# Scores and transposed scores of banded attention on two halves of TensorE's rows

## The reference, cut to what matters

```python
qkv = jnp.einsum('btc,oc->bto', x, w_qkv)
q, k, v = (heads(q), heads(k), heads(v))
attn = jnp.einsum('bhqd,bhkd->bhqk', q, k) / math.sqrt(DK)     # DK = 8
mask = jnp.abs(idx[None, :] - idx[:, None]) > WINDOW           # WINDOW = 128
attn = jnp.where(mask[None, None], -1000000000.0, attn)
p = jax.nn.softmax(attn, axis=-1)
out = jnp.einsum('bhqk,bhkd->bhqd', p, v)
```

## Time and profile before

| | |
|---|---|
| median of 3 runs | 1789.28 us |
| the profiled execution's own time | 1788.06 us |
| its span, first to last instruction | 1786.3 us |
| PE busy | 1529.7 us (86%) |
| DVE busy | 1484.7 us (83%) |
| ACT busy | 1265.5 us (71%) |
| POOL busy | 1328.8 us (74%) |
| mean granted clock of TensorE, of full speed | 0.963 |

### The profile page before, as it was taken

The page is one execution under the profiler, slowest core; times in us unless marked ns, Lnnn a source line. Parts: engine busy times, 40 slices in busy tenths (PEclk is TensorE's granted clock), DMA queues, the critical chain, the costliest instruction groups (busy, mean ns, idle before and its releaser), DMA issues.

```text
span 1786.3 us, 37722 instructions
## 1 busy us (share of the span) xinstructions
PE 1529.7 (86%) x11712; PEld 1086.0 (61%) x11712; DVE 1484.7 (83%) x3720; ACT 1265.5 (71%) x1741; POOL 1328.8 (74%) x1579
## 2 busy tenths in 40 slices
PE   3899999999999999868888888888888888888887
PEld 2456555555565556436666666666666666666666
DVE  3768888887888887339999999989899899899998
ACT  1156666666666666648888888888798888888885
POOL 1145555555555555649999999999999999999993
PEclk9789999999999999969999999999999999999999
DMA  5334444444444443110000000000000000000000
GB/s 139 84 83 93 103 98 97 97 96 96 105 96 96 98 104 75 40 40 1 19 19 1 19 18 6 12 18 18 1 18 18 8 11 18 18 0 18 13 7 7
DMA packets 73406, 85.14 MB, mean 48 GB/s; under 512 B 9856, under 2 KB 63616, under 8 KB 68608
## 3 DMA queue, kind: packets, MB, share of 16 engines
q1 hardware_dynamic: 73312, 84.08, 20.1%
HBM read 58.10 MB, written 25.95 MB: 47 GB/s over the span
## 4 chain that ended last, share of the span: by engine, by line
issue 20%; POOL 20%; DVE 7%; ACT 6%; PE 3%; DVEq 0%; POOLq 0%; ACTq 0%; SPq 0%
POOL SUM L751 20%; DVE W L944 5%; ACT E L852 4%; PE WT L1012 1%; ACT L786 1%; DVE M8Y L888 1%; PE MB L979 1%; PE E L967 1%; ACT GE L785 0%; DVE SMALL L905 0%; DVE CT L927 0%; ACT SIM L779 0%; ACT L785 0%; PE MB L954 0%; DVE Z L911 0%
## 5 line engine op out<-in xcount | busy, mean ns | idle before, releaser
L751 POOL TENSOR_TENSOR SUM<-SIM 128x1024 f32<-128x1024 f32 x512 | 958.3, 1920 | 16.5 <-DVE W L944 12.5
L944 DVE SCALAR_TENSOR_TENSOR W<-SUM,SMALL,E 128x1024 f32<-128x1024 f32 x512 | 642.7, 1280 | 52.3 <-ACT E L852 48.2
L852 ACT ACTIVATE E<-SUM,NB 128x1024 f32<-128x1024 f32 x512 | 567.4, 1118 | 112.8 <-DVE W L944 102.5
L1012 PEld LDWEIGHTS WT<-idf,W 128*128 128x128 f32 x4096 | 473.7, 146 | 263.3 <-DVE W L944 141.3
L1012 PE MATMUL WT<-idf,W 128*128 128x128 f32 x4096 | 552.6, 284 | 90.2 <-DVE CT L927 50.7
L264 POOL TENSOR_SCALAR_AFFINE_SELECT PT<-PT 128x128 f32<-128x128 f32 (+1 forms) x1024 | 334.5, 351 | 315.9 <-ACT PT L354 279.4
L409 DVE TENSOR_REDUCE mx<-SX 128x2 f32<-128x512 f32 x256 | 175.3, 685 | 104.7 <-PE SX L492 104.0
L411 DVE TENSOR_REDUCE mx<-SY 128x2 f32<-128x768 f32 x256 | 242.5, 947 | 6.8 <-PE SY L492 6.2
L354 ACT ACTIVATE PT<-TX 128x512 f32<-128x512 f32 x256 | 152.9, 597 | 95.7 <-PE TX L519 94.1
L356 ACT ACTIVATE PT<-TY 128x768 f32<-128x768 f32 x256 | 207.2, 809 | 1.4
L488 PE MATMUL SY<-K,Q 72*128 72x384 bf16 x512 | 163.2, 341 | 17.2 <-DVE mx L411 16.6
(11 more groups left out here) (111 smaller groups left out, 1663.1 us busy)
## 6 DMA issues: line engine op xcount, KB each, us to landing
K<-k_parts SPq DMA_DIRECT2D x96, 192.0 KB
Q<-q_parts SPq DMA_DIRECT2D x288, 64.0 KB
q_parts<-qp SPq DMA_DIRECT2D x16, 384.0 KB, 2.4
k_parts<-kp SPq DMA_DIRECT2D x16, 384.0 KB, 2.4
xin<-in_x SPq DMA_DIRECT2D x16, 256.0 KB, 3.1
xres<-in_x SPq DMA_DIRECT2D x16, 256.0 KB, 9.4
x<-X SPq DMA_DIRECT2D x16, 256.0 KB, 2.2
x2T<-X2T SPq DMA_DIRECT2D x16, 256.0 KB, 2.1
```

The source lines that it names most:

```text
L751: return eng.tensor_tensor(SUM[(q * FH + h) % RING][:, :].rearrange("p (i j) -> p i j", i=NK), sx, sy, ALU.add)
L852: nc.scalar.activation(E[h % 2][:, :], SUM[(k * FH + h) % RING][:, :], ACT.Exp, bias=NB[q][:, h:h + 1]).then_inc(S["exp_ready"], 1)
L944: nc.vector.scalar_tensor_tensor(out=W[h % WRING][:, :], in0=SUM[(k * FH + h) % RING][:, :], scalar=TOP[q][:, h, TOPK - 1:TOPK], in1=E[h % ...
L1012: o = pe.matmul(WT[:, e, :], W[h % WRING][:, e * P:(e + 1) * P], ident[:, :], is_transpose=True, start=(h == 0 and e % 4 == 0), stop=(h == ...
```

## The change: two halves of the array, other loads, other queues

- A product is taken as 6 terms, not 9 (the parts whose orders add up to two at most), so a score tile contracts over 48 rows, and the transposed one over 51.
- Q and K hold these 48 rows twice, from row 0 and from row 64. The scores of SX and of SY's first tile contract over the upper rows (0 to 47), the transposed scores and SY's second tile over the lower (64 to 114). `heads` writes the matmuls of both in turns. Each mask product over 128 rows becomes two over 64 rows: for SX two of 192 columns on the upper half, for SY two of 2 x 128 columns on each half.
- `values` is cut in four: at each head one of the four spans, 4 matmuls. VSLOT, ASLOT and SHARED move with it.
- SP stores each row where a load wants it (`store_rows`, 3 DMAs for q and 3 for k, 768 KB each, where there was 1 of 384 KB each), and a half is loaded by 4 DMAs of 48 rows, 384 KB each.
- The rows of maxima are stored and loaded from ScalarE's queue, the store one head before the load. `shift` is cut in pieces that lie one head apart. ScalarE now runs a head's exponentials ahead of the other work of that head, and the two short `pow`s of GpSimd lie one head later. `x2_stats` (L468 before) moves to head 1 of the next step.
- The loop of steps begins one step later, with a body of two steps as before.

```diff
-TERMS = 9
-KQ = TERMS * DK
+TERMS = ((0, 3), (1, 2), (2, 1))
+KQ = DK * sum(n for _, n in TERMS)
 SHIFT = 3
+HALF = P // 2
+LOADS = 16 * 4
+STORES = 16 * len(TERMS)
 HT = H // 2 * TILES
 TWO_ONES = float(np.array([0x3F803F80], np.uint32).view(np.float32)[0])
 SLOT_V = 32
 SLOT_PT = 1280
-VSLOT = ((6, 1), (10, 1), (14, 1), (2, 2))
-ASLOT = (3, 8)
+VSLOT = ((4, 1), (8, 1), (12, 1), (0, 2))
+ASLOT = (6, 8)
...
-    SHARED = [(1, "mt1", -1, "max_rest", 2, 2), (3, "att0", -2, "att_normed", 2, 1), (4, "xnT", 1, "xnT_ready", 1, 1),
-              (5, "q", 1, "q_rest", 1, 1), (7, "k", 1, "k_rest", 1, 1), (8, "att1", -2, "att_normed", 2, 2),
+    SHARED = [(1, "mt1", -1, "max_rest", 2, 2), (4, "xnT", 1, "xnT_ready", 1, 1), (5, "q", 1, "q_rest", 1, 1),
+              (6, "att0", -2, "att_normed", 2, 1), (7, "k", 1, "k_rest", 1, 1), (8, "att1", -2, "att_normed", 2, 2),
...
+            for r in (0, HALF):
+                sp.dma_start(K[b][r:r + KQ, hs, :], k_rows[:, hs, :]).then_inc(to, 16)
+                sp.dma_start(Q[b][r:r + KQ, hs, :], q_rows[:, hs, :]).then_inc(to, 16)
+        def store_rows(parts, rows, copies, done):
+            at = 0
+            for e, n in TERMS:
+                src = parts[:, e:e + 1, :].broadcast_to([P, n, T]) if copies else parts[:, 0:n, :]
+                sp.dma_start(rows[at:at + DK * n].rearrange("(a d) h n -> (d h) a n", a=n), src).then_inc(done, 16)
+                at += DK * n
...
-            if 0 <= c - 1 < SEQS:
-                await_(sp, S["max_part3"], (t - 1) * 2 + 2)
-                shift_rows(t - 1, 1, (c - 1) % 2)
...
-            for a in range(3):
-                sp.dma_start(K[b][24 * a:24 * a + 24, hs, :],
-                             k_parts.rearrange("a (d h) n -> (a d) h n", h=H)[:, hs, :]).then_inc(to, 16)
-                for e in range(3):
-                    r = 24 * a + 8 * e
-                    sp.dma_start(Q[b][r:r + 8, hs, :],
-                                 q_parts[a].rearrange("(d h) n -> d h n", h=H)[:, hs, :]).then_inc(to, 16)
...
+                store_rows(qp, q_rows, True, S["q_stored"])
...
+                store_rows(kp, k_rows, False, S["k_stored"])
+                await_(sp, S["q_stored"], STORES * (t + 2))
+                await_(sp, S["k_stored"], STORES * (t + 2))
...
-                if h == 1 and 0 <= c + 1 < SEQS:
+                if h == 2 and 0 <= c + 1 < SEQS:
...
-                if h == 13 and 0 <= c - 2 < SEQS:
+                if h == 14 and 0 <= c - 2 < SEQS:
...
-                    shift(t - 1, 2)
+                    shift_part1(t - 1, 2)
+                if h == 2 and 0 <= c - 1 < SEQS:
+                    shift_part2(t - 1, 2)
                 if h == 9 and 0 <= c < SEQS:
-                    shift(t, 1)
+                    shift_part1(t, 1)
+                if h == 10 and 0 <= c < SEQS:
+                    shift_part2(t, 1)
+                if h == 3 and 0 <= c - 1 < SEQS:
+                    store_shift(t - 1, 1)
+                if h == 4 and 0 <= c - 1 < SEQS:
+                    load_shift(t - 1, 1, (c - 1) % 2)
+                if h == 11 and 0 <= c < SEQS:
+                    store_shift(t, 0)
+                if h == 12 and 0 <= c < SEQS:
+                    load_shift(t, 0, c % 2)
...
-                    if g % 2 and h == sl and 0 <= c - ds_ < SEQS:
+                    if g % 2 and h == sl + 3 and 0 <= c - ds_ < SEQS:
...
+        def store_shift(s, half_):
+            hs = slice(8 * half_, 8 * half_ + 8)
+            await_(act, S["max_part3"], s * 2 + half_ + 1)
+            act.dma_start(m_parts[:, hs, :].rearrange("r h (i n) -> (h i) r n", n=P), mp[:, :, :]).then_inc(S["max_parts_stored"], 16)
+        def load_shift(s, half_, b):
+            hs = slice(8 * half_, 8 * half_ + 8)
+            await_(act, S["max_parts_stored"], 16 * (s * 2 + half_ + 1))
+            act.dma_start(Q[b][HALF + KQ:HALF + KQ + SHIFT, hs, :], m_parts[:, hs, :]).then_inc(S["max_rows_loaded"], 16)
...
+        ROWS_A, ROWS_B = slice(0, HALF), slice(HALF, P)
+        def heads(t, c, h):
+            scores, scoresT = 0 <= c < SEQS, 0 <= c - 1 < SEQS
+            n, m = t * H + h + 1, (t - 1) * H + h + 1
+            q, k, qT, kT = Q[c % 2], K[c % 2], Q[(c - 1) % 2], K[(c - 1) % 2]
+            def tile(out, r, i, k0, k1, clear=True):
+                pe.matmul(out, q[r:r + KQ, h, i * P:(i + 1) * P], k[r:r + KQ, h, k0 * P:k1 * P],
                           start=clear, stop=False, skip_group_check=True)
+            def outside(out, rows, low, band_):
+                return pe.matmul(out, idb[rows, low, :], bandb[rows, low, band_], start=False, stop=True, skip_group_check=True)
+            def tileT(out, j, q0, q1):
+                r = slice(HALF, HALF + KQ + SHIFT)
+                return pe.matmul(out[:, 0:(q1 - q0) * P], kT[r, h, j * P:(j + 1) * P], qT[r, h, q0 * P:q1 * P],
                                  start=True, stop=True, skip_group_check=True)
+            if scores and h == 0:
+                pe.wait_ge(S["heads_0_7_loaded"], LOADS * (t + 1))
+            if scores and h == 8:
+                pe.wait_ge(S["heads_8_15_loaded"], LOADS * (t + 1))
+            if scoresT and h == 0:
+                pe.wait_ge(S["max_rows_loaded"], 32 * (t - 1) + 16)
+            if scoresT and h == 8:
+                pe.wait_ge(S["max_rows_loaded"], 32 * (t - 1) + 32)
+            sx = SX[:, :, :].rearrange("p j n -> p (j n)")
+            if scores:
+                if c > 0 or h > 0:
+                    pe.wait_ge(S["outer_maxima"], n - 1)
+                tile(SX[:, 0, :], 0, 0, 0, 2)
+            if scoresT:
+                if c > 1 or h > 0:
+                    pe.wait_ge(S["outer_exp"], m - 1)
+                tileT(TX[:, 0, :], 0, 0, 2)
+            if scores:
+                tile(SX[:, 1, :], 0, 3, 2, 4, False)
+            if scoresT:
+                tileT(TX[:, 1, :], 3, 2, 4).then_inc(S["outer_scoresT"], 1)
+            if scores:
+                outside(sx[:, P:P + 192], ROWS_A, 0, slice(0, 192))
+            if scoresT:
+                if c > 1 or h > 0:
+                    pe.wait_ge(S["inner_exp"], m - 1)
+                tileT(TY[:, 0, :], 1, 0, 3)
+            if scores:
+                outside(sx[:, P + HALF:3 * P], ROWS_A, 1, slice(HALF, 2 * P)).then_inc(S["outer_scores"], 1)
+            if scoresT:
+                tileT(TY[:, 1, :], 2, 1, 4).then_inc(S["inner_scoresT"], 1)
+            if scores:
+                if c > 0 or h > 0:
+                    pe.wait_ge(S["inner_maxima"], n - 1)
+                tile(SY[:, 0, 0:3 * P], 0, 1, 0, 3)
+                tile(SY[:, 1, 0:3 * P], HALF, 2, 1, 4)
+                for low in range(2):
+                    for i, rows in enumerate((ROWS_A, ROWS_B)):
+                        ends = SY[:, i, :].rearrange("p (a n) -> p a n", n=2 * P)[:, :, 0:P]
+                        o = outside(ends, rows, low, slice(P, 3 * P))
+                        if low:
+                            o.then_inc(S["inner_scores"], 1)
...
+        def values(s, c, g, j):
...
+            at, q0, q1 = SPAN[j]
+            for e in range(4):
+                h, slot = 4 * g + e, g % 2 * VSUB + (j * 8 + g // 2 * 4 + e) * SLOT_V
+                o = pe.matmul(PV[32 * e:32 * e + 32, q0 * P:q1 * P], V[b][:, slot:slot + SLOT_V],
+                              PT[:, h % 8, at:at + (q1 - q0) * P], start=(j == 0 and g % 2 == 0), stop=(j == 3 and g % 2 == 1),
+                              skip_group_check=True)
+            if j == 3:
+                o.then_inc(S["values_product"], 1)
...
-                    if h == sl and 0 <= c - ds_ < SEQS:
-                        values(t - ds_, c - ds_, g)
-                if 0 <= c - 1 < SEQS:
-                    scoresT(t, c, h)
+                    if sl <= h < sl + 4 and 0 <= c - ds_ < SEQS:
+                        values(t - ds_, c - ds_, g, h - sl)
...
```

211 lines of the change are left out of this document (82 added, 129 removed).

## The result

The change made the kernel slower: 1858.79 us (median of five runs, 1854.42 to 1869.45) against 1789.74 before in the same runs, a ratio of 1.0395 [1.0363, 1.0426] (in brackets, here and below, the 95% interval). 1716 us, with a range of 1680 to 1768, had been forecast.

The account below looks back on a forecast made before the run. PE was taken to bound the kernel, DVE second. Steps 4.1 us shorter give 61.5 us over 15, plus start 5, step 0 4 and step 16 3: 73.5 us off 1789.28, thus 1716 us, range 1680 to 1768.

Parts of the forecast that it names:

- Two halves: Score matmuls on PE: pairs on upper and lower rows overlap fully, a head takes 0.94 us, 8.0 us less a step.
- Rivals 1 and 3: Halves on PE: 1, partial overlap or growing waits, 1756 us, chance 0.13; 3, no overlap, 1885 us, chance 0.08.
- Work per step: Steps 1 to 15: PE has 35.0 us of work a step, and DVE's stays at 35.04.
- The 3.1 us for switches: Value products on PE, now at 16 heads: 12 more round trips into column groups cost 3.1 us a step.
- Waits that remain: Handovers between engines in each step: waits and unevenness add 4.0 us to 35, so a step takes 39.0.
- The pow: The `pow` of trs on GpSimd, behind head 14's masks: a wait of 1.0 us a step.
- a longer stop at ACT's wait: ACT's load of the maxima waiting for its store: a stop costing over 4 us a step, chance 0.02.
- covered: Loads of Q and K: a half lasts 8 us at 200 GB/s and is there at 32 to 34 of 39 us.
- The start: PE's first scores wait for Q: 4 even loads instead of 12 save about 5 us.
- step 0: First step, a hand-over of SX and SY between PE and DVE: fewer SY columns gain 4 us.
- rival 2: Loads too late at 91 GB/s: PE stands at head 0, the start wins nothing, 1765 us, chance 0.07.
- Rival 4, the clock: Steps 1 to 15 stay at 1.2 GHz: PE's 35 us become near 65, time over 2000 us, chance 0.03.

Follow-up runs that it names:

- e5: e4 with transposed scores, SY's second tile and its mask also on the upper rows, so no pairs on different halves: 2049.5 us, ratio 1.1406.
- e4: The changed kernel with ScalarE's loads of the maxima later, steps written out without a loop, and GpSimd's pow ahead of head 14's masks: 1755.0 us, ratio 0.9799.
- e14: e4 with the loads of heads 0 to 7 cut in two, heads 0 to 3 first, same bytes: 1716.5 us, ratio 0.9595.
- e13: e4 with half of the Q and K loads left out from sequence 2 on, and a group's value products at one head again: 1777.1 us, ratio 0.9937.
- e1: The changed kernel with only ScalarE's loads of the maxima moved later, from heads 4 and 12 to 6 and 13: 1822.9 us, ratio 1.0171.
- e3: The changed kernel with GpSimd's pow for x1 ahead of head 14's masks, not behind them: 1834.4 us, ratio 1.0236.
- e15: The changed kernel with late loads of the maxima and the pow first, as in e4, but the loop kept: 1802.5 us, ratio 1.0072.
- e11: Control: the kernel before the change with its steps written out, no loop: 1787.2 us, ratio 0.9978.

## Why the prediction was wrong, by its steps

**Two halves: right.** 0.94 us a head was taken. SX to SX with the values between is 1.82 us in the fence above, of which the values take 0.78 (402.81 to 403.59); the head is left with 1.04, a switch in it. Rivals 1 and 3 are refuted by the starts and by `e5`, where a head without the overlap takes 1.81 us (1.72 was taken for it).

**Work per step: right.** PE 35.0 and DVE 35.04 were taken, 35.7 and 35.6 of busy time measured in `e4`, and 39.4 us a step in `e14` against a forecast of 39.0. PE's sum was made from starts and busy time holds tails as well (40.23 for a sum of 38.3 before), so the terms are confirmed together and not one by one. The 3.1 us for switches was never measured alone. The Trainium skill (TensorEngine Tiling, "Key Properties") says that changing the mode drains TensorE. `e13` shows only that this is worth less here than what lumps make DVE wait.

**"Waits that remain": the first step that failed.** 1.0 us a step was taken for ACT's wait for its own store, by a store that lands in 2.4 us with nothing ahead. That row is of 384 KB of q; the store of the maxima has 24 KB, and beside two or three loads it took 5.1 to 7.9 us. ACT stood for it up to 5.7 us, 43.5 us in 11 waits (the two rows above), 2.9 a step. The prediction looked at head 12, beside the loads of the next sequence. The larger part is at head 4, ahead of xnT (31.9 us in 8), where the loads of heads 8 to 15 are under way: in the step shown SP issued them from 409.17 on, the store followed at 416.89. The range went to 6, and the value was chosen too near its lower end. The pow was put at 1.0 and cost PE 2.2. A price was given to the wait alone, not to the clock after it. `e1` and `e3` take out 40 and 28 us. The case of "a longer stop at ACT's wait" had 0.02.

**Code: a term that the sum did not have.** The sum has nothing for the loop's turns. `e15` against `e4` gives 49 us for its four turns, and `e11` 4 us before the change. In the Trainium skill (Runtime: NRT & Kernel Launch, "Instruction fetch mechanics") stands that a taken branch to a place outside of what the engine holds must fetch it and stalls. The stops of 3 to 6 us at the turns and the 78 packets (36 before) agree with it; before the change the queue was silent at the same branch.

**DMA: "covered" was wrong.** A half was to be there at 32 to 34 us of a step. In the step of `e4` that begins at 287.62, its loads start at 28.1 us, not at 24, and PE goes on 13.4 us after that, not 8, at 41.5: it waited 1.97 us at head 0. The start gained nothing in the changed kernel, since a whole half, 1.57 MB now, must land before head 0 (PE's first wait for Q was 14.04 us, 11.35 in the earlier trace rows). Nor did step 0, which ends with a wait of 3.50 us for Q. A wait at head 0 and a start that wins nothing were forecast for rival 2, whose cause (91 GB/s) is not what happened. The order of the heads cures it: 37 us from `e4` to `e14`, the start's 5 and some 5 of step 0 among them.

**Rival 4, the clock: right in kind, wrong in its condition.** It asked for "gaps that a step with PE at 90% doesn't have". The step wasn't at 90%, because of the stops, and behind the stops the work ran slow as well (0.56 to 0.59 at 424 to 428 us, 0.50 at 456 to 472). In step 16 the clock stayed down though PE was busy 39.98 of 40 us.

**The sign.** With the three stops out and the loads in quarters the same change gives 1716.5 us, which was the forecast. That the numbers meet is in part luck. It is no proof of the prediction, since `e14` is not the kernel that was priced, and terms cancel: its step 16 gave 7 us where 3 were taken, and `ffn` lost 2.8 where nothing was. Mechanism and work were right; the error is that four gaps of 2 to 6 us each were priced at 1 us or at nothing.

**Open.** Why the clock does not come back in step 16 and is 0.80 in the middle of `e5`. The kind of work alone doesn't decide it: `e3` ran the same step 16 at 1.00, and `e5` the same steps at 1.00 from 400 to 560 us. Which engine's code makes the stop at the turn, and whether the length of the body is what makes it, was not tried. Nor was it tried why the loads move half of what the stores do with the DMA engines full.

## What to carry to other kernels

When two engines are balanced to within some per cent, look at the longest single stop that the change can make, not at the average wait: a stop of over 2 us was paid once in time and again in the clock after it. A DMA that an engine waits for in its own program must be priced with the transfers that are under way beside it, and issued so early that these don't matter. And where a change makes the program longer, look whether the loop's turn still passes without a fetch.
